# Renewing a rotation table eight tiles before the next layer, one slot at a time

## The reference

```
q = l2norm(q) * q_scale[l];  k = l2norm(k) * k_scale[l]
q = q * cos * scale + rotate_half(q) * sin * scale
k = k * cos / scale + rotate_half(k) * sin / scale
```

## Time and profile before

| | us |
|---|---|
| median of 3 runs | 3965.4 (3961.76 to 3970.67) |
| the profiled execution, its time | 3970.83 |
| its span in the profile | 3969.0 |
| DVE busy, of that span | 3427.1 (86%) |
| PE busy | 3711.0 (93%) |
| ACT busy | 3283.5 (83%) |
| POOL busy | 2394.3 (60%) |

### The profile page before, as it was taken

How to read it: one execution, slowest core, us unless ns; L and a number is a source line. 1 busy time by engine, 2 the same in 40 slices (tenths; PEclk the granted TensorE clock), 3 DMA queues, 4 the chain that set the end, 5 groups by cost and what they waited for, 6 DMA issues and landing times.

```text
span 3969.0 us, 124299 instructions
## 1 busy us (share of the span) xinstructions
PE 3711.0 (93%) x49248; PEld 2334.9 (59%) x49248; DVE 3427.1 (86%) x7048; ACT 3283.5 (83%) x9269; POOL 2394.3 (60%) x1468
## 2 busy tenths in 40 slices
PE   5999999976999999999999999999999999999996
PEld 2444444433666666666666666666666666666664
DVE  6999999957888988889888888988989889898894
ACT  3999999964888888888888888888888888888884
POOL 2444433435766767667676666766767667676672
PEclk7999999987999999999999999999999999999998
DMA  1000000001222323223232232322323223232321
GB/s 50 3 9 11 12 9 21 17 1 38 79 82 77 97 81 84 82 75 99 80 85 82 76 95 79 88 77 81 97 79 86 78 80 98 81 86 79 84 79 54
DMA packets 129599, 263.07 MB, mean 66 GB/s; under 512 B 34944, under 2 KB 36736, under 8 KB 128768
## 3 DMA queue, kind: packets, MB, share of 16 engines
q1 hardware_dynamic: 129024, 255.16, 23.0%
HBM read 26.43 MB, written 2.10 MB: 7 GB/s over the span
## 4 chain that ended last, share of the span: by engine, by line
PE 48%; ACT 23%; DVE 16%; issue 7%; POOL 4%; DMA 2%; SPq 2%; DVEq 0%; ACTq 0%; POOLq 0%
PE ps L667 12%; ACT arena L954 12%; PE ps L739 6%; PE ps L611 5%; PE ps L606 5%; PE ps L552 4%; PE ps L547 3%; ACT arena L941 3%; ACT arena L946 2%; DVE arena L1255 2%; DVE arena L1176 2%; PE ps L798 2%; DVE arena L1169 2%; DVE ssq L1197 2%; PE ps L748 2%
## 5 line engine op out<-in xcount | busy, mean ns | idle before, releaser
L954 ACT ACTIVATE arena<-arena,nmx 128x64 f32<-128x64 f32 x3072 | 1024.9, 340 | 42.3 <-DVE arena L1255 40.3
L497 POOL TENSOR_TENSOR arena<-arena,rinv 128x1024 f32<-128x1024 f32 x192 | 365.3, 1902 | 622.3 <-DVE rinv L1228 622.3
L667 PE MATMUL ps<-WB,arena 128*128 128x512 f32 x1152 | 572.4, 620 | 50.3 <-ACT arena L969 30.5
L667 PE MATMUL ps<-WN,arena 128*128 128x512 f32 x1152 | 560.1, 608 | 38.3 <-ACT arena L969 30.8
L954 ACT ACTIVATION_READ_ACCUMULATOR arena<-arena,nmx 128x1 f32 x3072 | 594.5, 194 | 0.0
L930 ACT ACTIVATE arena<-ps 128x1024 f32<-128x1024 f32 x384 | 392.1, 1021 | 227.6 <-PE ps L667 222.0
L481 POOL TENSOR_TENSOR arena<-arena 128x1024 f32<-128x1024 f32 x192 | 454.3, 2366 | 182.1 <-DVE arena L1169 162.1
L1176 DVE TENSOR_TENSOR arena<-ps,tables 128x512 f32<-128x512 f32 x768 | 490.1, 678 | 18.7 <-ACT arena L930 18.5
L486 POOL TENSOR_TENSOR arena<-arena 128x1024 f32<-128x1024 f32 x192 | 453.6, 2362 | 50.7 <-DVE arena L1169 47.1
L739 PEld LDWEIGHTS ps<-arena 128*64 128x64 f32 x12288 | 379.6, 139 | 164.2 <-issue 132.0
L1169 DVE TENSOR_TENSOR arena<-ps,tables 128x1024 f32<-128x1024 f32 x384 | 459.4, 1196 | 0.0
(11 more groups left out here) (113 smaller groups left out, 7104.5 us busy)
## 6 DMA issues: line engine op xcount, KB each, us to landing
arena<-arena SPq DMA_DIRECT2D x1536, 64.0 KB
arena<-arena SPq DMA_DIRECT2D x192, 384.0 KB, 3.4
arena<-arena SPq DMA_DIRECT2D x192, 128.0 KB, 3.5
arena<-X SPq DMA_DIRECT2D x96, 128.0 KB, 3.1
arena<-Y SPq DMA_DIRECT2D x96, 128.0 KB, 3.1
WB<-wb SPq DMA_DIRECT2D x15, 512.0 KB, 5.8
arena<-wa SPq DMA_DIRECT2D x8, 581.0 KB, 3.7
WN<-wb SPq DMA_DIRECT2D x9, 512.0 KB, 4.6
```

Source lines behind the costliest of these rows:

```text
L667: i = pe.matmul(banks[:, c, :], x, W[:, w * INNER + c * COL:w * INNER + (c + 1) * COL], start=True, stop=True)
L954: i = act.activation(pe3[:, :, h, :], sc[:, 64 * h:64 * h + 64].rearrange("p (k q) -> p k q", k=2), ACT.Exp, bias=nmx[:, h:h + 1], accum_o ...
```

## The change

`tables_of` stays for layer 0, in step -1. For every later layer, the new `table_of(t)` renews one slot of `tables` (all four kinds, 4 x 64 = 256 elements in each partition, both inputs in SBUF) in one DVE operation. It comes behind `maxima`, at the end of the step that rotated the last tile to use this slot: steps s = 32 l + 23 to 32 l + 30, that is with s+1 = 24 to 31 in the layer, in each of the first five layers. The step that opens a layer only waits for the eight operations. The scales are loaded in step s = 32 l - 16, behind a wait for the last use of the former ones.

```
@@ SP
             def scales_in(l):
-                need(sp, tab_r, 4 * l)
+                need(sp, tab_r, 4 + TS * (l - 1) if l else 0)
                 weights(l, B_SC, B_W, ls)
@@ SP, step s
-                if live(s + 2) and (s + 2) // NT > 0 and (s + 2) % NT == 0:
-                    scales_in((s + 2) // NT)
+                if 0 < (s + 16) // NT < LAYERS and (s + 16) % NT == 0:
+                    scales_in((s + 16) // NT)
@@ DVE
+            def table_of(t):
+
+                if t % NT == 0:
+                    dve.wait_ge(ls, 16 * (t // NT + 1))
+                scales = WB[:, B_SC:B_SC + 4 * DH].rearrange("p (i d) -> p i d", i=4)
+                dve.tensor_tensor(tables[:, :, t % TS, :], rotary[:, :, t % TS, :], scales, ALU.mult).then_inc(tab_r, 1)
@@ DVE, step s, at its start
-                if live(s + 1) and (s + 1) % NT == 0:
-                    tables_of((s + 1) // NT)
+                if s == -1:
+                    tables_of(0)
+                if s > 0 and live(s + 1) and (s + 1) % NT == 0:
+                    dve.wait_ge(tab_r, 4 + TS * ((s + 1) // NT))
@@ DVE, step s, behind maxima(s)
+                if live(s + 1 + TS) and (s + 1 + TS) // NT > (s + 1) // NT and s >= -1:
+                    table_of(s + 1 + TS)
```

## The result

| | before | changed |
|---|---|---|
| median of 9 runs | 3966.31 us (3961.76 to 3970.67) | 3978.28 us (3970.7 to 3983.06) |
| ratio | | 1.0028, 95% interval 1.0019 to 1.0038 |
| span of the profiled execution | 3969.0 | 3975.2 |

The change makes the kernel slower by 12 us, with a 95% interval of 7.5 to 15. The forecast was +18 (3983, range 3968 to 3996). One execution of the kernel of experiment 10 took 17670 us, more than four times any other; its ratio leaves that one out.

A forecast was written before the change was run, and what follows sets the result against it. No engine bounds the kernel by itself; DVE is packed except at the Gelu wait. Removal returns 24.8 us and added operations cost 42.8, so +18.0 on the 3965.4 median gives 3983 us, range 3968 to 3996.

The forecast's parts named there:

- The removal: Five `tables_of` blocks of 5.08 us at layer starts vanish: 25.4 us, less 0.6 for the new wait, net 24.8.
- The added operations stand still for L490: Behind `maxima`, each of 40 `table_of` operations waits for POOL's L490 to end, lasting about 1.25 to 1.7 us.
- The rival of the small operation that slips through: Operations of 256 elements don't wait for L490, costing 0.34 us each at 30 places: -14.6 us, 3951; chance 0.09.
- The tail after L490: DVE's next operation starts 0.20 us after L490 ends; 0.34 if nothing is hidden behind the wait.
- What is covered: Shifts behind s % 4 = 3, 0, 1, 2 remain as 1.45, 1.35, 0.3 and 1.18 us: 4.28 a cycle, 42.8 in all.
- The Gelu wait: DVE's 2.57 us wait before L1278 for ACT's Gelu absorbs about 1.0 of the 1.30 shift behind s % 4 = 1.
- The rival of no cover: At the Gelu wait nothing is absorbed, 1.0 us more at 10 places: +28 us, 3993; chance 0.12.
- more cover than I see: Small DVE waits for PE, ACT and POOL absorb more of the shift: +6 us, 3971; chance 0.12.
- the likeliest case: The sum of +18 us with its own range, +13 to +25 us, 3978 to 3990; forecast chance 0.67.
- the Gelu places: Shifts behind s % 4 = 1, before the Gelu wait, leave 0 to 0.7 us each in the likeliest case's range.
- the longer tail: Tail of 0.34 us instead of 0.20 after L490, raising the sum by up to 4 us.
- The scales and SP: SP's five loads issued 14 steps earlier cost nil; the 0.4 us gain is already in the 25.4.

The follow-up runs named there:

- experiment 10: Kernel of experiment 9 with the two small operations ending the feed-forward statistics made `tensor_reduce` instead of `tensor_scalar`; 3933.05 us, ratio 0.9909.
- experiment 1: Changed kernel without the 40 table operations and their wait where a layer opens, so the removal alone; 3940.29 us, ratio 0.9936.
- experiment 5: Changed kernel with each of the 40 operations renewing one of four kinds, 64 elements instead of 256, same place; 3973.42 us, ratio 1.002.
- experiment 2: Changed kernel with the same 40 operations moved from behind `maxima` to behind `norms` of the same step; 3942.3 us, ratio 0.9942.
- experiment 6: Changed kernel with the 40 operations replaced by a `tensor_reduce` of 256 elements with one SBUF input, same place; 3948.25 us, ratio 0.9958.
- experiment 7: Changed kernel with each renewal split into two operations of 128 elements, one behind the other; 4051.46 us, ratio 1.022.
- experiment 4: Kernel before the change with only the early load of the scales, step 32 l - 16 instead of 32 l - 2; 3968.13 us, ratio 1.0006.
- experiment 8: Changed kernel with an operation of the same shape and place in every step of the first five layers, 120 more; 4090.16 us, ratio 1.0314.
- experiment 3: Kernel before the change with the 40 table operations issued by POOL between `add_q` and `unit_k`, scales loaded early; 3943.76 us, ratio 0.9945.
- experiment 9: Kernel of experiment 2 with `final` of the last layer also moved from behind `maxima` to behind `norms`; 3932.7 us, ratio 0.9918.

## Why the prediction was right, and where its size was off

**The removal.** Summed at 25.4 less 0.6; experiment 1 gives 25.8. That the block of four was 5.08 long because of two standstills and passed on whole is right: without it and without the new operations (experiment 1), the step that opens layer 2 is 4.95 us shorter and the two behind it 0.1 together.

**The added operations stand still for L490.** Right in every part that a run can show. The durations were forecast at 1.7, 1.7, 1.4 and 1.25 us behind s % 4 = 3, 0, 1 and 2, and are 1.83, 1.83, 1.38 and 1.26 in the timeline above. Elements hardly matter (experiment 5), the place beside POOL does (2), the second SBUF input or the kind of operation does (6), and a further operation waits for a further POOL operation (7). The rival of the small operation that slips through is excluded by these and by L1223 above: its one long run, of 128x32, met POOL's L486 and lasted 2.37 us. These are DVE and POOL of the changed kernel there:

```profile
937.72 2.37 DVE L1223 TENSOR_TENSOR nwt<-rinv 128x32 f32<-128x32 f32 x1
```

```profile
937.70 2.35 POOL L486 TENSOR_TENSOR arena<-arena 128x1024 f32<-128x1024 f32 x1 [0.79 <-PE ps L699]
```

By the Trainium skill's page "SBUF — State Buffer", section "Who interferes with whom", the order of issue and not the shape decides which of the two engines blocks the other, and the traces agree: 32, 64, 128 and 256 elements all waited.

**The tail after L490**, 0.20 by the rows, is 0.20 to 0.21, and 0.00 with 64 elements in 32 of the 40 of experiment 5. The rule of the Trainium skill's page "VectorE: DVE Perf Modes", section on the TRN2 errata, with nothing hidden behind the wait, would have made it 0.34: the measurement decides for the rows.

**What is covered.** From `maxima` to `maxima` of steps 58 to 62 the changed kernel takes 1906.87 - 1841.71 = 65.16 us; before it was 1902.45 - 1841.37 = 61.08, so +4.08 for the cycle; by the regular lengths it is 4.3 (16.67 + 14.67 + 19.49 + 14.35 = 65.2 against 60.9). The forecast was 4.28. By its terms, behind s % 4 = 3, 0, 1 and 2: 1.26 to 1.38 (forecast 1.45), 1.44 (1.35), 0.2 to 0.4 (0.3) and 1.04 to 1.16 (1.18). The Gelu wait gave the 1.0 that was expected of it, 2.57 to 1.50. The rival of no cover is excluded.

**The sum, +18 against +12.** With 4.28 a cycle by the regular lengths, ten cycles and the return of 24.8, the forecast's 18 is right for the regular steps. The median moved by 12, and experiment 1 puts the difference into the added operations: they cost 38 us and not the 42.8 of the sum. The failed term is the one that I took as nothing: the cover by late steps. The rival "more cover than I see", with a chance of 0.12 and a price of 12 us, holds in part, by about 5 us, though in another way than I wrote: it spoke of small waits in every step. My rows came from regular steps. The run also has late ones, and a DVE that is 1.0 to 1.4 later anyway covers them. Over the last eight steps of the five layers (40 steps from `maxima` to `maxima`), the time over the median of the same step in the five layers is 7.1, 7.1 and 3.5 us in three traces without the operations there (before, experiments 1 and 4), and 1.1, 1.3, 0.9 and 0.6 in four with them (changed, 5, 7 and 8). The difference of the means is 5 us. With short operations or POOL's it is 3.8, 2.2 and 3.8 (experiments 2, 3 and 6), so single traces scatter by 2 us or more, and the clearest proof is experiment 8, with three times as many further steps. 18 - 5 leaves +13, inside the interval of 7.5 to 15.

The time lies in the wide range. The range of the likeliest case, +13 to +25, began above the measured +12; by its own terms (the Gelu places and the longer tail) it would have been +15 to +26. In times that range is 3978 to 3990, and that the measured 3978.28 just reaches it is luck: the median before, now of nine runs, is 0.9 above the one that the forecast started from.

**The scales and SP.** Nothing that can be told, as forecast (experiment 4, within 6 us).

**Was the change worth anything?** Its idea was: the renewal off the start of a layer gives 25.8 us, and the price can be made nearly nil. The place behind `maxima` gave it all away and 12 more. Experiments 2, 3 and 9 keep it.

## What to carry to other kernels

Before an elementwise DVE operation with two SBUF inputs is moved or split, look at what POOL runs at the new place: here the same 40 operations cost 38 us beside POOL and 2 us three or four places earlier. Busy time hides this: a DVE operation that stands still for POOL is shown as busy, so compare a line's longest and shortest duration for one shape. And a microsecond saved on an engine that looks packed can come back as a wait two steps on, while a microsecond added there is paid: test both directions before summing up savings.

## What was not expected of the hardware

**A tiny operation can stand still as well.** L1279, a `tensor_scalar` with one SBUF input and four elements in each partition, meets POOL's L481 in 46 of its 48 runs. Then it lasts 0.72 to 1.22 us and ends 0.02 to 0.03 behind L481; the two others take 0.17. As a `tensor_reduce` it takes 0.157 every time. In experiment 3 a `tensor_scalar` of 128x32 ended with POOL's operation in the same way.

**A lower granted clock of PE is beside some late steps, and not most.** In the kernel before, PE stood idle for 2.00 us, and the next products of L667 took 3.62 us for four (1.88 to 1.98 in the 65 us before). The windows view, with the busy time of each engine and then the granted clock (PEclk):

```profile
2176.00:2181.00 5.00, 3.68 (x8) 1.30 (x10) 4.71 (x14) 3.06 (x14) 3.08 (x3) 0.66 0.53 160
```

```profile
2177.32 3.62 PE L667 MATMUL ps<-WB,arena 128*128 128x512 f32 x4 [2.00 <-issue]
```

The granted clock of 0.66 over 5.00 us means that for 3.4 us PE ran at the lower of its two levels, 1.2 GHz instead of 2.4. The two steps there, from `sumsq` to `sumsq`, are 1.1 and 1.7 us longer than others of their kind. In experiment 8 the same thing happened, behind an idle time of 2.27:

```profile
2236.80:2240.20 3.40, 2.66 (x3) 1.17 (x4) 3.13 (x12) 1.86 (x10) 1.48 (x2) 0.56 0.89 260
```

```profile
2237.54 3.50 PE L667 MATMUL ps<-WB,arena 128*128 128x512 f32 x4 [2.27 <-issue]
```

Here no step was more than 0.5 us over its kind's median; a later DVE covers it, as far as these two can show. Why PE waited for its queue there ("issue") none of the runs shows.

The clock isn't what makes most steps late. Of the nine late ones in the kernel before, four lie in such a stretch or right behind it, and five have none near. The changed kernel has four late steps and none near a low stretch, and the trace of experiment 3 has seven and no low stretch in layers 1 to 4 at all. The late steps stand at nearly the same tiles in every trace but that of experiment 8 (the one from the `sumsq` of tile 82 to that of tile 83 is 1.1 to 1.7 us late in eleven of twelve traces), so they belong to the program and aren't chance; what they wait for is open.
